# A gated linear attention with eight experts: three changes of the array's form in a step with late transposes, residuals placed beside the sorted rows, scatters that only write

## The reference, cut to what matters

```python
xn = (x - mean(x)) / sqrt(var(x) + 1e-5)
q, k = xn @ Wq, xn @ Wk                       # 4 heads of 32
v, g = xn @ Wv, xn @ Wg                       # 4 heads of 64
gk   = log_sigmoid(xn @ Wgk + bgk) / 16       # one decay per head and row
gc   = cumsum(gk) in chunks of 64 rows
A    = (q * 32**-0.5) @ k.T * exp(gc_t - gc_s), lower triangle, in a chunk
o    = A @ v + (q * exp(gc)) @ S              # S: state carried from chunk to chunk
S    = exp(gt) * S + (k * exp(gt - gc)).T @ v
attn = (o * rsqrt(mean(o*o) + 1e-5) * gnorm_w * silu(g)) @ Wo

p = softmax(xn @ gate_w)                      # 8 experts, the best one is used
e, w = argmax(p), max(p)
ffn = w * (gelu(xn @ w1[e] + b1[e]) @ w2[e] + b2[e])
out = x + attn + ffn
```

## Time and profile before

| | us |
|---|---|
| median of 3 runs (lowest, highest) | 389.59 (389.52, 390.5) |
| the profiled execution's own time | 389.28 |
| its span in the trace | 387.5 |
| busy in the span: PE, DVE, ACT, POOL | 373.4, 314.5, 291.8, 279.1 |
| mean granted clock of the matrix engine | 0.994 |

### The profile page before, as it was taken

How to read it: one execution, slowest core, us unless ns; L and a number is a source line. 1 busy time by engine, 2 the same in 40 slices (tenths; PEclk the granted TensorE clock), 3 DMA queues, 4 the chain that set the end, 5 groups by cost and what they waited for, 6 DMA issues and landing times.

```text
span 387.5 us, 13901 instructions
## 1 busy us (share of the span) xinstructions
PE 373.4 (96%) x3963; PEld 321.2 (83%) x3963; DVE 314.5 (81%) x859; ACT 291.8 (75%) x889; POOL 279.1 (72%) x245
## 2 busy tenths in 40 slices
PE   7999999999999999999999999899999999999992
PEld 7667777777777877787777877899999999999991
DVE  5988999989898988888888878777788787777761
ACT  4889987788888888888888886566666667666661
POOL 8003534878787888888788873288888888888886
PEclk9999999999999999999999999999999999999997
DMA  8946788456555445575654423155555455556440
GB/s 231 257 140 198 223 270 292 134 170 191 170 184 161 138 147 157 158 200 162 191 157 150 131 79 81 54 67 72 64 72 70 65 70 71 69 71 76 75 37 6
DMA packets 59106, 51.45 MB, mean 133 GB/s; under 512 B 7200, under 2 KB 51392, under 8 KB 59072
## 3 DMA queue, kind: packets, MB, share of 16 engines
q1 hardware_dynamic: 45936, 42.07, 38.8%
q0 software_dynamic: 12272, 8.54, 15.3%
q10 hardware_dynamic: 864, 0.40, 0.4%
HBM read 33.14 MB, written 18.30 MB: 133 GB/s over the span
## 4 chain that ended last, share of the span: by engine, by line
PE 83%; DVE 4%; DMA 3%; issue 3%; ACT 2%; POOL 2%; SPq 2%; DVEq 0%; ACTq 0%; POOLq 0%
PE psA L988 16%; PE psVG L976 15%; PE psVG L771 11%; PE psT L867 8%; PE psO L825 7%; PE psQK L757 5%; PE psT L851 4%; PE psVG L790 4%; PE psO L839 3%; PE psKS L814 3%; POOL out_dram L619 2%; SPq L355 2%; DMA x_all<-in_L_attn_x_dram 1%; ACT E L1160 1%; DMA gcB<-decay_rows 1%
## 5 line engine op out<-in xcount | busy, mean ns | idle before, releaser
L619 POOL DMA_INDIRECT out_dram<-yw,sidx x71 | 112.9, 1590 | 28.8 <-DVE sidx L1700 17.5
L1160 ACT ACTIVATE E<-gcB,ngc 128x128 f32<-128x128 f32 x256 | 78.3, 395 | 0.7 <-DMA gcB<-decay_rows 0.7
L577 POOL DMA_INDIRECT sorted_rows<-x_all,pos_i x64 | 64.9, 1015 | 13.4 <-issue 12.8
L561 POOL TENSOR_TENSOR rms<-msn,neg_half 128x8 f32<-128x8 f32 x32 | 54.4, 1699 | 26.5 <-DVE msn L1492 22.5
L554 POOL TENSOR_SCALAR_AFFINE_SELECT E<-E 128x1024 f32<-128x1024 f32 x32 | 35.2, 1099 | 36.5 <-ACT E L1160 24.9
L1142 ACT ACTIVATE th<-psVG,x_all 128x256 f32<-128x256 f32 x64 | 26.9, 470 | 20.4 <-issue 11.6
L988 PE MATMUL psA<-xT_all,v_sb 128*128 x288 | 38.3, 276 | 1.0 <-issue 0.6
L976 PE MATMUL psVG<-xgT,gcB 128*128 128x128 f32 x288 | 37.9, 275 | 0.0
L988 PE MATMUL psA<-xT_all,th 128*128 x280 | 37.4, 276 | 0.0
L976 PE MATMUL psVG<-xgT,E 128*128 128x128 f32 x280 | 37.0, 275 | 0.0
L867 PE MATMUL psT<-wo_sb,oT 128*128 128x128 f32 x256 | 36.9, 287 | 0.0
(11 more groups left out here) (214 smaller groups left out, 950.6 us busy)
## 6 DMA issues: line engine op xcount, KB each, us to landing
gcB<-decay_rows SPq DMA_DIRECT2D x32, 512.0 KB
sorted_rows<-blank SPq DMA_DIRECT2D x12, 396.0 KB, 5.0
xg<-sorted_rows SPq DMA_DIRECT2D x71, 66.0 KB
x_all<-in_L_attn_x_dram SPq DMA_DIRECT2D x16, 256.0 KB, 5.2
out_dram<-res SPq DMA_DIRECT2D x32, 128.0 KB
eqB<-decay_exp_rows SPq DMA_DIRECT2D x32, 64.0 KB
w1b<-in_L_ffn_w_dram SPq DMA_DIRECT2D x8, 256.0 KB
xT_all<-in_L_ffn_w_dram SPq DMA_DIRECT2D x32, 64.0 KB
```

What stands on the lines that cost most here:

```text
L561: nc.gpsimd.tensor_tensor(rms[j][:], msn[j][:], neg_half[:, 0:2 * H], ALU.pow).then_inc(rms_ready, 1)
L577: nc.gpsimd.indirect_dma_start(out=sorted_dram, out_offset=bass.IndirectOffsetOnAxis(ap=pos_i[:, t:t + 1], axis=0), in_=x_all[:, t, :], in ...
L619: nc.gpsimd.indirect_dma_start(out=out_rows, out_offset=bass.IndirectOffsetOnAxis(ap=sidx[j][:], axis=0), in_=yw[j][:], in_offset=None, bo ...
L1160: last = nc.scalar.activation(E[j][:, k, h * P:(h + 1) * P], gcB[j][:, k * H + h, :], ACT.Exp, bias=ngcf[:, bass.ds((s * 2 + k) * H + h, 1)])
```

## The change

1. **Step on PE.** The transposes are those of s-2 and stand behind q and k. v and g come ahead of the scores. The scores go into `psA` and the free halves of `psKO` (the former `psKS` and `psO` as one tile), not into `psVG`. The output projection is made in two halves of 64 array columns, behind the scores. The state is stored next to the keys' transposes and waits for the first half of the probabilities; the outputs take the heads in pairs. PE's loop over the steps is unrolled.
2. **ACT and DVE.** ACT copies q and k first and does the exponentials in two halves, the second behind the copy of v; `qk_sb` has two buffers. DVE gates, decays the keys, takes the mean square and scales q ahead of the probabilities.
3. **Rows.** `x_all` gets 128 columns more, a tile's xT, which the residual x + attn overwrites later. A row of `sorted_rows` is now 260 elements, 1040 bytes: x, four terms, residual. Twice as many clears of nearly the same size (24 of 128 x 780) fill it, five of them at once behind the loads of x. Tiles 0 to 53 are placed whole when their residual is there. Tiles 54 to 63 are placed in halves: x first, the residuals (`place_res`) from step 30 on and behind the last step. SP stores no residuals. The second layer's weights lie over the first 32 tiles' part and wait until these are placed.
4. **Experts.** The scatters write x + attn + ffn without adding and wait for no store. `weigh` is split: `take` adds the bias out of PSUM, `weigh` follows one block later and adds the residual that was loaded with the row. For the first eight blocks the second halves of the rows are loaded apart, and `weigh(0,0)` stands behind `take(0,4)` and waits for all eight.

The diff, cut to its core:

```diff
@@ SP
+            sp.wait_ge(blank_made, 2)
+            for k in range(5):
+                clear(k)
             store_decays(0)
...
+            sp.wait_ge(placed_low, EXP * FC * 16)
...
             def load_block(i, j):
                 b = i * R + j
+                sp.wait_ge(y_out, b - R + 1)
                 sp.dma_start(xg[j][:], sorted_dram[bass.ds(b * P, P), :]).then_inc(xg_loaded[j], 16)
...
+            sp.wait_ge(placed, (TILES - EXP * FC) * 16)
+            for j in range(R):
+                sp.dma_start(xg[j][:, 0:XH], sorted_dram[j * P:(j + 1) * P, 0:XH]).then_inc(xg_loaded[j], 16)
+            sp.wait_ge(res_placed, (TILES - WHOLE) * 16)
+            for j in range(R):
+                sp.dma_start(xg[j][:, XH:XR], sorted_dram[j * P:(j + 1) * P, XH:XR]).then_inc(xr_loaded, 16)
@@ POOL
             def place_rows(t):
                 pool.sem_inc(tick, 1)
+                if t < WHOLE:
+                    pool.wait_ge(res_ready, t // 2 + 1)
...
+                    nc.gpsimd.indirect_dma_start(out=half_rows, out_offset=bass.IndirectOffsetOnAxis(ap=half_i[:, 0, t - WHOLE:t - WHOLE + 1], axis=0),
+                                                 in_=x_all[:, t, 0:XH], in_offset=None).then_inc(placed, 16)
+            def place_res(t):
+                pool.wait_ge(res_ready, t // 2 + 1)
+                nc.gpsimd.indirect_dma_start(out=half_rows, out_offset=bass.IndirectOffsetOnAxis(ap=half_i[:, 1, t - WHOLE:t - WHOLE + 1], axis=0),
+                                             in_=x_all[:, t, XH:XR], in_offset=None).then_inc(res_placed, 16)
...
+                if s * 2 - 6 >= WHOLE:
+                    place_res(s * 2 - 6)
+                    place_res(s * 2 - 5)
...
+            for t in range(SEQS * 2 - 4, TILES):
+                place_res(t)
...
-            for j in range(2):
-                pool.wait_ge(res_stored[j], SEQS // 2 * 16)
...
-                                             in_=yw[j][:], in_offset=None, bounds_check=TOKENS - 1, oob_is_err=False,
-                                             compute_op=ALU.add).then_inc(scattered[j], 16)
+                                             in_=yw[j][:], in_offset=None, bounds_check=TOKENS - 1, oob_is_err=False).then_inc(scattered[j], 16)
@@ PE
             def scores(i, j):
                 s = i * 2 + j
                 pe.wait_ge(p_ready, s * 2)
-                pe.wait_ge(gate_ready, s + 1)
+                pe.wait_ge(og_ready, s)
+                pe.wait_ge(s_copied, s)
+                pe.wait_ge(kd_ready, s + 1)
...
             def project_out(i, j):
...
+                        for c in range(2):
+                            last = nc.tensor.matmul(psT[c * P // 2:(c + 1) * P // 2, k * D:(k + 1) * D], oT[:, 2 * k + a, c * P // 2:(c + 1) * P // 2],
+                                                    wo_sb[:, a, :], start=(a == 0), stop=(a == 1), skip_group_check=True)
...
                 first_keys(i, j)
                 proj_qk(*turn(i, j, 1, 2))
+                transpose_on(*turn(i, j, -2, 2))
+                proj_vg(*turn(i, j, 1, 2))
                 scores(i, j)
                 project_out(*turn(i, j, -2, 2))
                 if extra:
                     extra()
-                proj_vg(*turn(i, j, 1, 2))
                 state(i, j)
                 if ahead_of_outputs:
                     ahead_of_outputs()
                 outputs(i, j)
-                transpose_on(*turn(i, j, -1, 2))
@@ DVE
+            def take(i, j):
+                b = i * R + j
+                dve.wait_ge(y_ready, b + 1)
...
+                nc.vector.tensor_tensor(yb[j], psY[j % 2][:, 0:D], wbuf[j % 4][:, FF + FC:WB], ALU.add).then_inc(y_taken, 1)
...
             def weigh(i, j):
                 b = i * R + j
+                if isinstance(i, int) and i == 0:
+                    dve.wait_ge(xr_loaded, R * 16)
...
+                nc.vector.scalar_tensor_tensor(yw[j][:], yb[j], xg[j][:, D + 2:D + 3], xg[j][:, XW:XR], ALU.mult, ALU.add).then_inc(y_out, 1)
...
-            weigh(0, 0)
+            take(0, 0)
             residual(last, 1)
-            e = block_step(0, 1, e)
-            for j in range(2, R):
+            done = 0
+            for j in range(1, R):
                 e = block_step(0, j, e)
+                while done < WEIGHED_BY[j]:
+                    weigh(0, done)
+                    done += 1
...
+WHOLE = 54
+W2_FROM = 10
+WEIGHED_BY = [0, 0, 0, 0, 1, 3, 5, 7]
```

More of the change, by code:

```diff
@@ L254, in build_layer @@
         gcB_loaded = [sem(f"gcB_loaded{j}") for j in range(2)]
-        res_stored = [sem(f"res_stored{j}") for j in range(2)]
         xg_loaded = [sem(f"xg_loaded{j}") for j in range(R)]
@@ L429, in _ @@
             sp.wait_ge(eq_stored[1], 16)
-            for j in range(2):
-                for k in range(4):
-                    clear(4 + j * 4 + k)
-                step(2, j)
+            for k in range(15, 19):
+                clear(k)
+            step(2, 0)
+            for k in range(19, CLEARS):
+                clear(k)
+            step(2, 1)
+            sp.dma_start(w1b[:, :, FF + FC:WB], b2.partition_broadcast(P)).then_inc(w_loaded, 16)
             with sp.Fori(3, 3 + EXP // 2) as i:
@@ L475, in _ @@
                 load_block(TURNS - 1, j)
-            for j in range(2):
-                sp.wait_ge(res_stored[j], SEQS // 2 * 16)
         @block.gpsimd
@@ L833, in outputs @@
                     pe.wait_ge(og_ready, s)
-                own_half(i, j, 0)
-                own_half(i, j, 1)
+                first, second = (0, 1) if isinstance(i, int) and s in BY_HALVES else (1, 0)
+                pe.wait_ge(p_ready, s * 2 + 1)
+                own_pair(i, j, first, True)
+                pe.wait_ge(p_ready, s * 2 + 2)
+                own_pair(i, j, second, False)
                 pe.wait_ge(s_copied, s + 1)
@@ L952, in _ @@
             step(2, 1)
-            with pe.Fori(3, SEQS // 2 - 1) as i:
+            for i in range(3, SEQS // 2 - 1):
                 for j in range(2):
@@ L1462, in slots_to_positions, with half_positions @@
                 late(nc.vector.tensor_copy(pos_i[:], pos[:]))
+            def half_positions():
+                for a in range(2):
+                    late(nc.vector.tensor_scalar(half_f[:, a, :], pos[:, WHOLE:TILES], 2.0, float(a), ALU.mult, ALU.add))
+                late(nc.vector.tensor_copy(half_i[:], half_f[:]))
             def scale_wo():
@@ L1664, in _ @@
             step(3, 1, aside=block_experts)
-            step(4, 0)
+            step(4, 0, behind=half_positions)
             step(4, 1)
@@ L1769, in placed_by, with placed_in @@
     return n
+def placed_in(s):
+    whole, part = 0, WHOLE
+    for k in range(PLACE_FROM, s + 1):
+        tiles = []
+        for _ in range(placed_by(k) - placed_by(k - 1)):
+            if whole < min(WHOLE, (k - 2) * 2):
+                tiles.append(whole)
+                whole += 1
+            else:
+                tiles.append(part)
+                part += 1
+    return tiles if s >= PLACE_FROM else []
 ROUTE = {"az0": 4, "g0": 5, "gdiff0": 7, "az1": 15, "g1": 16, "onehot": 21, "gdiff1": 23, "count": 24, "nb": 27, "all": 29}
```

266 lines of the change are left out of this document (136 added, 130 removed).

## The result

The changed kernel takes **432.53 us** in the median of four runs (425.83 to 434.27); the kernel before took 389.55 in the four beside it. The ratio is 1.1005 (95% interval 1.0907 to 1.1104): slower by a tenth, where the forecast was 387.8 and the range ended at 394. The ratio takes fast runs alone, of the changed kernel 425.83, 429.0 and 431.82 out of six on record. The profiled run is the shortest, 425.83, with a span of 424.0; what longer runs lose on top was not profiled.

The account below looks back on a forecast made before the run. TensorE (PE) was taken to bound the kernel. Steps −10.1, start +2.5, passage +1.8, read-back +6.1, clock +1.5 and tail −3.3 sum to −1.5: 389.28 becomes 387.8 us, range 380.5 to 394.

Parts of the forecast that it names:

- The step on PE: Attention steps: a step falls from 6.50 to 6.15 us, −10.1 us over the 29 middle steps (bounds 0 and −13.3).
- the two terms: Per step on PE: fewer changes of array form, −0.15 us, and stalls that go, −0.20 us.
- the loop's branch: PE's loop branch leaves 0.22 us at the start of even turns; unrolling removes it, part of the −0.20 for stalls.
- that rival: Output projection: half-width projections take half the time, 0.45 us less on PE, stopped by POOL's 5.94; 381.7 us, chance 0.07.
- The rival in which POOL becomes the bound: Steps: longer rows make placements exceed 1.10 us, so POOL sets the step; 393.6 us at 1.20, chance 0.15.
- The experts: Experts' stage: a block takes 1.90 us, which the change leaves as it is; 0 for blocks 10 to 70.
- The start: Before the steps: five clears in SP's queue hold the decays' store by 0 to 5.0 us; +2.5 taken.
- The passage: From steps to experts: scores(31) wait for gated(30), and two placements stand ahead of rms(31); +1.8 us (bounds 0 and +4).
- The read-back: First expert blocks: weigh(0,0) waits for all second halves, delaying block 8's rows; PE stands 4.9 us; +6.1 (bounds 0 and +8).
- the clock: Experts: during the stand at block 8 PE's clock may fall; +1.5 us (bounds 0 and +4).
- The tail: Behind PE's last matmul: scatters without adding take 1.01 us, so POOL's backlog goes; −3.3 us (bounds 0 and −3.3).
- The sign that the prediction named for being wrong: A step stays near 6.5 us with PE waiting for POOL or DVE, or PE never stands at block 8.

Follow-up runs that it names:

- e6: Changed kernel without its 54 whole placements (a semaphore is counted up in their place; nearly all scatter rows are skipped): 414.13 us, one run.
- e2: Kernel before with PE's loop over steps 6 to 29 unrolled, nothing else changed: 388.75 us, ratio 1.0015.
- e5: Changed kernel whose 54 whole placements write 528-byte rows, without the residual, into another tensor that nobody reads: 428.37 us, one run.
- e3: Kernel before with the attention's part of the change alone; rows, adding scatters, residual stores and clears as before: 401.19 us, ratio 1.0304.
- e4: Changed kernel with scatters that add to the output's rows again: 420.92 us, ratio 1.0807.
- e7: Kernel before with scatters that only write, nothing else changed: 403.01 us, ratio 1.0345.
- e12: Changed kernel with its first five clears put back behind step 0's loads: 420.58 us, ratio 1.082.
- e11: Kernel before with the attention's part alone, x_lo behind the scaled queries, one placement moved behind POOL's mask, last scores by halves again: 390.23 us, ratio 1.0054.
- e1: Changed kernel with PE's steps 6 to 29 in a loop again, all else as changed: 421.83 us, ratio 1.086.

## Why the prediction was wrong, step by step

**The step on PE.** The sum of the two terms was right: 6.15 was forecast, 6.14 is every step of e6 from the tenth on; over all 29 it is −7.6 for the −10.1, since the steps ahead of the tenth are longer. How the sum divides was not shown: by itself the loop's branch, priced at 0.22 of every second step, is worth nothing, for the steps of e2 take 6.50 in the mean as before. From the first start to the last, sixteen half-width matmuls of the output projection take 0.82 us and eight of full width 0.88, as the 0 for them said, so that rival is out. The rival in which POOL becomes the bound had its sign, placements above 1.10, and yet e5's steps, with rows of 528 bytes, are as long. What failed is the sentence "New waits are covered: the scores now wait for the gating of s−1, the state's copy and the decayed keys, which DVE does first in its step, while PE has 1.5 us of projections more ahead of the scores". x_lo stands ahead of both in DVE's list, and the mask holds it for a further 1.06 (e3). Then the signals of the scores themselves come late, by up to 1.1 us, and those of the outputs by up to 1.9. I asked of POOL only whether its 5.94 us fit a step. Whom its transfers hold while they are issued I did not ask: the placements cost 201.08 − 184.36 = 16.7 us of the steps (e6), which turns −7.6 into +9.1. How the 16.7 divide between held signals and x_lo no run separates: x_lo lasts 0.88 us in the mean in the changed kernel and 0.70 in e6.

**The experts.** "In the experts' stage a block takes 1.90 us (256.06 to 257.96), which the change leaves as it is" is the second step that failed. The scatter's 1.01 us was right, and so was a backlog that goes; that the shorter transfer would hold PE's signals was no rival of mine. It costs 124.81 − 113.75 = 11.1 us of blocks 10 to 70 (e4), 11.8 in the kernel before (e7).

**The start.** Right in kind, mis-sized: +2.5 was the middle of 0 and 5.0. The start grew by 4.2; the five clears alone cost 5.7 to step 2 and 5.0 in the span (e12), which is at the upper bound and over it. The chain of waits of the changed kernel, which answers to the earlier trace rows, has the store later and longer:

```profile
20.46 5.67 DMA decay_rows<-gcT
```

It lands at 26.14, where it landed at 22.01. It did not overtake the clears. The section of the Trainium skill that the prediction draws on here (DMA: Bandwidth & Descriptors, HWDGE ordering) orders how descriptors are taken, not how transfers land, so "for certain" was more than it says.

**The passage.** +1.8 was +4.3. "scores(31) now wait for gated(30)" named the wrong wait. They also wait for the decayed keys, and those stand in DVE's list behind the first block's normalising, which waits for a load, and its weights:

```profile
250.45 0.35 DVE L1733 TENSOR_SCALAR xgn<-xg 128x128 f32<-128x128 f32 x1 [0.79 <-DMA xg<-sorted_rows]
250.71 0.49 DVE L1726 COPY gcB<-w1b 128x644 f32 x1
251.11 0.29 DVE L1565 TENSOR_TENSOR kd<-psKO,e_k 128x128 f32<-128x128 f32 x1
...
252.10 0.58 PE L800 MATMUL psKO<-qk_sb 32*128 32x128 f32 x2 [3.16 <-DVE kd L1565]
```

e11 bears it out: scores by halves wait for neither, and 2.1 us come back.

**The read-back.** Forecast 6.1 and 1.5 for the clock, measured +9.8. The mechanism is in the trace where it was put:

```profile
277.64 0.34 DVE L1750 SCALAR_TENSOR_TENSOR yw<-pr,xg 128x128 f32<-128x128 f32 x1
278.16 11.77 SPq L462 DMA_DIRECT2D xg<-sorted_rows  x7
...
280.93 0.34 DVE L1733 TENSOR_SCALAR xgn<-xg 128x128 f32<-128x128 f32 x1 [2.55 <-DMA xg<-sorted_rows]
281.33 0.33 PE L988 MATMUL psQK<-ident,xgn 128*128 128x128 f32 x1 [1.87 <-DVE xgn L1733]
```

The first weighing comes at 277.64, block 8's rows are asked for behind it, and PE stands for 1.87 at block 8 and 0.90 at block 9, with the granted clock at 0.57 over the two blocks, near the lower level, and 7.89 us in place of 3.79. The stand itself is shorter than the 4.9 forecast because PE had lost time ahead of it: behind block 4, while the last placements were issued, signals came up to 3.65 us late (that of a second layer that ended at 268.36 stands at 272.01). So the nearness of 7.6 to 9.8 is in part luck: from block 7 to block 10 it is 6.1, clock included; 2.5 are that stand behind block 4, which was no term of mine, and most of the rest lies between blocks 0 and 1, where its cause stays open.

**The tail.** −3.3 was −1.5: the last two blocks are both weighed at the end, so their scatters follow each other (420.07 and 421.36, 0.98 each), and the second starts 2.8 us behind PE's last result, not 1.5.

Against the forecast's terms: steps +19.2, experts +10.5, passage +2.5, read-back +2.2, tail +1.8, start +1.7; together 37.9, which with the forecast's −1.5 are the 36.4 of the table. The sign that the prediction named for being wrong came: the 29 steps take 6.93 in the mean, with PE waiting for DVE.

## What to carry to other kernels

An engine that has time to spare can still be in the way: before a transfer on GpSimd is made shorter, longer or moved, look in the trace at which signals of TensorE fall into its issue, and at who waits for them. Where engine B is idle long after engine A's instruction has ended, and A went on meanwhile, compare the end with the semaphore event; take the suspected neighbour away for one run to see whose it is. And a new wait is covered only if everything ahead of its producer in that engine's list is covered too.

## What was not expected of the hardware

A signal of TensorE that ends while GpSimd issues an indirect DMA that only writes (0.96 to 1.14 us) may be seen only behind that transfer's end, mostly 0.3 to 0.8 us, or, where two or three follow each other, behind the last: up to 3.65 us late, while TensorE's next instructions run on. Under an indirect DMA that adds (1.59 us), 0 of 78 and 1 of 103 signals were late. Neither the rows' length (528 or 1040 bytes, e5) nor whether they land matters: in e6, where nearly all rows of the scatters are skipped, 24 of 59 are late. Not every signal inside such a transfer is held. In four traces with scatters and placements that only write (after, e1, e5, e6; from 97 us on) it was 29 of 44 of those that ended about 0.25 us behind its start, and 1 of 39 at 0.05. Nor is it the instant alone: in the steps of e6 nine signals of the transposes end 0.24 to 0.30 us behind the start of a half placement, and none is late. What decides it, and why the adding form is free of it, these runs don't show.
